# Who issues the two small transfers of the negative row maxima in a two-layer attention and MLP kernel

## The reference

```python
mod = silu(condition) @ Wada + bada                      # layer 0
xm  = layernorm(x) * (1 + sc_a) + sh_a
scores = einsum('bhqd,bhkd->bhqk', q, k) * hd ** -0.5    # causal in layer 0
attn = softmax(scores) @ v
x = x + gt_a * (attn @ Wproj + bproj)
x = x + gt_m * (gelu(xm2 @ W1 + b1) @ W2 + b2)           # layer 1: the same, ungated
```

## Time and profile before

| | |
|---|---|
| median of 3 runs | 1156.61 us |
| the profiled execution's own time | 1153.95 us |
| its span, first to last instruction | 1152.1 us |
| outside the span | 1.85 us |
| granted TensorE clock, mean | 0.970 of full speed |
| PE, DVE, ACT, POOL busy | 93%, 68%, 54%, 22% |

### The profile page before, as it was taken

The page is one execution under the profiler, slowest core; times in us unless marked ns, Lnnn a source line. Parts: engine busy times, 40 slices in busy tenths (PEclk is TensorE's granted clock), DMA queues, the critical chain, the costliest instruction groups (busy, mean ns, idle before and its releaser), DMA issues.

```text
span 1152.1 us, 24600 instructions
## 1 busy us (share of the span) xinstructions
PE 1073.7 (93%) x8972; PEld 939.3 (82%) x8972; DVE 786.7 (68%) x2379; ACT 620.1 (54%) x1255; POOL 252.4 (22%) x253
## 2 busy tenths in 40 slices
PE   3979999999998689999996999999999978999998
PEld 3768889889886578999885888888888756988997
DVE  5468888888875577655636778787787746566553
ACT  1146666666665643433432777777777666344431
POOL 5111121212211343223411021211112013121111
PEclk9689999999999999999996999999999999999999
DMA  7556867576760100000069546555474400010001
GB/s 216 100 85 111 127 135 121 104 123 115 165 93 13 42 20 10 11 10 15 13 97 178 84 60 99 71 88 84 68 100 62 58 2 1 20 37 20 19 20 37
DMA packets 50833, 81.52 MB, mean 71 GB/s; under 512 B 8917, under 2 KB 23477, under 8 KB 49621
## 3 DMA queue, kind: packets, MB, share of 16 engines
q1 hardware_dynamic: 50232, 79.16, 39.5%
q10 hardware_dynamic: 480, 0.79, 0.6%
HBM read 22.64 MB, written 8.44 MB: 27 GB/s over the span
## 4 chain that ended last, share of the span: by engine, by line
PE 83%; DMA 5%; DVE 4%; ACT 2%; SPq 2%; issue 2%; POOL 2%; ACTq 0%; POOLq 0%; DVEq 0%
PE g_bank L564 14%; PE st_bank L564 14%; PE o_bank L652 9%; PE o_bank L564 7%; PE s_bank L564 7%; PE s_bank L619 6%; PE st_bank L638 5%; PE st_bank L632 4%; PE s_bank L615 3%; PE st_bank L634 3%; PE g_bank L710 2%; DMA k_stack<-qk_split 2%; SPq L423 2%; DMA q_stack<-negmaxT 2%; PE g_bank L718 1%
## 5 line engine op out<-in xcount | busy, mean ns | idle before, releaser
L833 ACT ACTIVATE probs<-st_bank 128x384 f32<-128x384 f32 (+1 forms) x512 | 273.5, 548 | 145.1 <-PE st_bank L634 78.6
L936 ACT ACTIVATE probs<-st_bank,cols 128x512 f32<-128x512 f32 x128 | 87.9, 688 | 214.5 <-PE st_bank L564 188.5
L564 PE MATMUL st_bank<-qk_split,q_stack 128*128 128x512 f32 x768 | 187.4, 402 | 15.8 <-ACT probs L936 11.2
L1129 DVE CUSTOM_DVE_ANT_0 s_bank<-s_bank,tri_wide 128x128 f32<-128x128 f32 (+1 forms) x512 | 170.4, 387 | 36.0 <-PE s_bank L616 34.7
L1135 DVE TENSOR_REDUCE maxima<-s_bank 128x2 f32<-128x512 f32 x256 | 168.8, 685 | 35.4 <-PE s_bank L619 34.6
L564 PEld LDWEIGHTS st_bank<-qk_split,q_stack 128*128 128x128 f32 x768 | 144.8, 191 | 53.5 <-ACT probs L936 14.7
L652 PE MATMUL o_bank<-probs,v_sb 128*32 128x256 f32 (+1 forms) x2048 | 124.9, 362 | 1.6 <-ACT probs L833 1.6
L564 PE MATMUL g_bank<-xmT,wa 128*128 128x256 f32 x768 | 121.7, 298 | 4.9 <-POOL xmT L1313 4.8
L619 PE MATMUL s_bank<-k_stack,q_stack 97*128 97x256 f32 x512 | 116.7, 313 | 3.8 <-DVE maxima L1135 1.9
L638 PE MATMUL st_bank<-q_stack,k_stack 99*128 99x256 f32 x512 | 104.5, 288 | 11.0 <-DMA q_stack<-negmaxT 10.2
L1313 POOL TENSOR_TENSOR xmT<-xm_full,xmT 128x512 fp32r<-128x512 f32 x32 | 42.3, 1323 | 329.9 <-ACT xmT L899 329.9
(11 more groups left out here) (113 smaller groups left out, 2071.2 us busy)
## 6 DMA issues: line engine op xcount, KB each, us to landing
q_stack<-qk_split SPq DMA_DIRECT2D x192, 128.0 KB, 4.6
k_stack<-qk_split SPq DMA_DIRECT2D x186, 128.0 KB, 6.2
gate_rows<-gate_dram SPq DMA_DIRECT2D x32, 128.0 KB, 3.2
w_dram<-w_in SPq DMA_DIRECT2D x8, 512.0 KB, 7.1
wm_f32r<-w_dram SPq DMA_DIRECT2D x4, 1024.0 KB, 12.8
out<-x_sb SPq DMA_DIRECT2D x8, 512.0 KB, 2.9
x_sb<-x_in SPq DMA_DIRECT2D x4, 512.0 KB, 7.0
q_stack<-q_stack SPq DMA_DIRECT2D x4, 384.0 KB
```

The source lines that it names most:

```text
L564: last = mm(dst, weights[i], rows[j], start=(f == 0 and n == 0), stop=(f == tiles - 1 and n == len(TERMS) - 1))
L833: activation(probs[:, h % 8, 0:n], st_bank[h % 2][:, 0:n], ACT.Exp, scale=SCALE)\
L936: activation(h_full[:, m % 2], st_bank[m % 2][:, :], ACT.Gelu, bias=cols[:, cb + m:cb + m + 1])\
L1129: last = v.tensor_tensor_reduce(out=bank[:, keys], in0=bank[:, keys], in1=tri_wide[:, T - (i + 1) * P:T], scale=1.0, scalar=LOWEST, op0=AL ...
```

## The change

The two transfers leave SP's program and stand in ACT's, directly behind ACT's copy. ACT first waits for the semaphore that its own copy raises. SP no longer waits for that semaphore. Sizes, destinations, sources and the semaphore that PE waits for are as before; the transfers now go through ACT's DMA queue.

```diff
@@ SP, step()
-                    g = in_layer(layer, c)
-                    when(negmaxT_copied, g.count(1, 1))
-                    for e in range(2):
-                        sp.dma_start(q_stack[ROW_MAX + e:ROW_MAX + e + 1, stack_of(g)].bitcast(fp32),
-                                     negmaxT[H * e:H * (e + 1)].bitcast(fp32)).then_inc(max_loaded[g.mod(2)], 16)
@@ ACT, step(), slot 1
                         activation(negmaxT[:], g_bank[0][0:32, 0:T], ACT.Copy).then_inc(negmaxT_copied, 1)
+                        act.wait_ge(negmaxT_copied, gc.count(1, 1))
+                        for e in range(2):
+                            act.dma_start(q_stack[ROW_MAX + e:ROW_MAX + e + 1, stack_of(gc)].bitcast(fp32),
+                                          negmaxT[H * e:H * (e + 1)].bitcast(fp32))\
+                                .then_inc(max_loaded[gc.mod(2)], 16)
                     if s == SLOT["q"][1] and a.within(B):
                         high(q_ready, q_hi, q_stacked, g_bank[1], q_split, 0)
```

## The result

The changed kernel took 1164.56 us in the median of 17 runs (1159.98 to 1174.74), the kernel before 1158.52 us in 17 runs beside it (1155.13 to 1163.55). The ratio is 1.0066, 95% interval 1.0045 to 1.0087: about 7.6 us slower, where 4.3 us was forecast.

A forecast was written before the change was run, and what follows sets the result against it. PE, busy for 93% of the span, was taken as the bound. The terms 6.8 + 0.3 + 2.3 - 4.7 - 0.4 = +4.3 us gave 1160.9 us, 0.37% slower, range 1154.5 to 1168.

The forecast's parts named there:

- The price of an issue on ACT: ACT's two issues: 0.58 us each as on SP, bounds 0.46 and 0.65; a block of 1.3 us.
- A full step of layer 1: 13 steps: high part of q 1.25 us late, head 2's maximum late, PE loses 0.52 us each, 6.8 us.
- The second way, through the restack: Late low part of q delays SP's restack 0.75 us; next step's first scores 0.5 us later, not added.
- A full step of layer 0: 12 steps: high part of q 1.15 us late, head 5's scores late, PE loses 0.12 us each.
- The first two steps of layer 0: Chain waits for restack of k; late low part of q costs 0.8 us for both, bounds nothing to 1.25 each.
- The first softmax of layer 1: Transfers no longer behind 2 MB of weights on SP's queue; landing 4 us after second issue, 4.7 us gained.
- the two rules weighed there: First softmax of layer 1: queues served in turn, gain 4 to 6.6 us; or spreading saves only issuing, nothing gained.
- the one against the change: Skill rule that spreading issues over engines saves only issuing time: nothing gained, sum 9 us slower, chance 0.17.
- The last two batches: Each layer's last two batches: PE waits for landing anyway, issues on an empty queue are shorter; gain 0.4 us.

The follow-up runs named there:

- The series of block lengths: Kernels in which ACT stands for different times: one 32 KB transfer, two DRAM copies, the change, three DRAM copies; layer 1's full steps lose 0.15, 0.27, 0.56, 0.83 us.
- the copies to DRAM: Kernel before, transfers left on SP, ACT also issuing two or three copies of negmaxT to scratch DRAM; ratios to before 1.0018 and 1.0147.
- DVE's order: Changed kernel with DVE's low part of q placed behind the maximum of head 2; ratio to before 1.0092.
- behind the high part: Changed kernel with ACT's wait and two issues placed behind its high part of q; ratio to before 1.0001.
- one transfer: Changed kernel with one 32 KB transfer for both rows in place of two of 16 KB, on ACT; ratio to before 1.0021.

## Why the prediction was right, point by point

The direction, the range (1154.5 to 1168) and most of the mechanism held. The size was 4.3 us where 7.6 was measured.

- **The price of an issue on ACT** was taken as 0.58 us from SP and measured at 0.59; the delay of the high part of q as 1.25 us and measured at 1.20. Right.
- **A full step of layer 1**: forecast a loss of 0.52 us by way of DVE's low part of q and the maximum of head 2, measured 0.56 us, and the chain of waits names that way. The series of block lengths gives a spare time of 0.55 to 0.65 us; the prediction's own figures had 0.73.
- **The second way, through the restack**: forecast as equally late. In full steps of the changed kernel PE never waited for it; only with DVE's low part of q later still did seven short waits come. The way is real, its equal weight wasn't shown, and since the two were not added the sum doesn't depend on it.
- **A full step of layer 0**: forecast 0.12 us, measured 0.14 us. (12 x 0.12 + 0.8 is 2.24 us, where the prediction's sum has 2.3.)
- **The first two steps of layer 0**: 0.8 us was forecast for both, by a later restack of k. In the first, PE's wait for it is 2.4 to 2.7 us in the six kernels in which the high part of q is on time there, and 3.4 to 3.7 us in the four that send all maxima through ACT ahead of it (2.9 and 3.3 with the copies to DRAM): 1.1 us more after the change. The length of that step says less. It was 19.27 us before and 22.12 after, but 21.18 us in a kernel unchanged there and 19.46 us when that kernel was run again, at mean granted clocks of 0.94, 0.81, 0.82 and 0.95. All six kernels with a block had such a dip of the clock behind this wait, and two of the six without one; whether the longer wait brings it on is open. The second step took 20.31 us before and 21.16 after, at 1.00 and 0.97, and can't be told apart from that.
- **The first softmax of layer 1**: this is the term that was mis-sized. "I take 4 us from the second issue ... and 4.7 us are gained": the landing took 6.51 us and the step became 2.9 us shorter. And the reason given, that ACT's queue is served beside SP's, earned nothing that can be told where it was tried alone. Of the two rules weighed there, the one against the change was nearer what that kernel showed. That the changed kernel still came out 2.9 us shorter there is luck as far as the prediction goes: the weights landed sooner, as told below.
- **The last two batches**: forecast a gain of 0.4 us. The one step between their copies took 18.77 us in layer 0 against 19.09, and 20.62 us in layer 1 against 18.88; one issue on ACT took 1.49 us there. Over all kernels it follows the clock: 16.9 to 17.7 us at a mean granted clock of 1.0, 18.5 to 19.5 at 0.91, 20.3 to 20.7 at 0.83. Beside that a gain of 0.4 us can't be seen.

Without the 4.7 us the sum of the prediction was 9.0 us, and with the measured 2.9 us in its place 6.1.

What stays open: why the step behind layer 1's first softmax is 23.2 to 23.5 us in three kernels in which ACT issues everything and SP loads the weights early (the change, DVE's order, behind the high part) and 21.6 us in the fourth (one transfer), but 26.0 us in the one in which ACT issues only that batch's two, and 25.5 and 25.6 us with the copies to DRAM. The traces show what it goes with. In all eight kernels with early weights PE went on 0.5 to 1.8 us after the second weight transfer had landed, whichever queue carried the maxima. That landing came 3.9 to 6.7 us behind the copy's start in the first four, and 7.1 to 8.6 us in the other four, the kernel before among them; counted from the first weight issue it came after 13.1 to 17.1 us and 17.4 to 20.1 us. Why the weights are through sooner wasn't isolated, so no part of the 2.9 us is shown to be the second queue's work.

## What to carry to other kernels

An issue of a transfer on a computing engine costs the engine its 0.6 us only as far as the engine has no work handed over to it meanwhile. Place it behind an activation whose inputs are there (the high part of q here), so that the sequencer issues while the engine computes; directly behind the producer, with a wait for it, everything queued behind stands still, and an idle share of 46% on that engine does not help. To get a small transfer past a large one, move the large one: a second queue gained nothing that could be told, where issuing the 2 MB behind the small ones took 5.0 to 5.5 us off that step, put 0.6 to 1.0 us on the next, and was worth 3.6 and 5.7 us of the whole kernel.

## What the runs showed that was not expected

- The same 16 KB out of `negmaxT` is issued on ACT in 308 ns (the first of two) and 439 ns (the second) towards DRAM, and in 511 and 608 ns towards a row of one partition in SBUF, all in the median.
- One transfer of 32 KB for both rows costs one issue of 622 ns, where the two small ones cost 1.16 us together; PE's weight loads then waited for its landing in five full steps of layer 1, 0.2 to 0.3 us each, against two with the two small ones.
- With the engines full of 8 KB pieces, the two transfers of 16 pieces of 1 KB each, on an otherwise empty queue, started mostly 3.3 us after their issue and landed after 8.0 us. In ordinary steps it is 1.1 us and 2.2 us.
- The time between runs of one kernel varies by 5 to 15 us, and the profiles show dips of the granted clock that sit in other stages from one to the next. A loss of 0.14 us a step could be read only by steps.
